# Attention output projection: plain fp32 products in place of three products of split halves

## What is computed

```python
def _L0_attn_ref(x, Wq, Wk, Wv, Wo):
    ...
    attn = jax.nn.softmax(scores, axis=-1).astype(x.dtype)
    ctx = jnp.einsum('bhgtk,bhkd->bhgtd', attn, v)
    out = ctx.reshape(b, H, t, DH).transpose(0, 2, 1, 3).reshape(b, t, E)
    return out @ Wo.T
...
h = _layernorm(x, axis=-1) * (1 + ca) + sa
x = x + ga * _L0_attn_ref(h, L0_attn_Wq, L0_attn_Wk, L0_attn_Wv, L0_attn_Wo)
h = _layernorm(x, axis=-1) * (1 + cb) + sb
x = x + gb * _L0_ffn_ref(h, ...)
```

## Time and profile before

| | |
|---|---|
| median of 3 runs | 870.54 us (870.29 to 873.26) |
| the profiled execution | 873.01 us |
| its span, first to last instruction | 871.0 us |
| PE busy | 750.3 us (86%), 4006 matmul records |
| DVE busy | 524.8 us (60%) |
| ACT busy | 331.0 us (38%) |
| POOL busy | 245.9 us (28%) |
| mean granted TensorE clock | 0.939 |

### The profile page before, as it was taken

How to read it: one execution, slowest core, us unless ns; L and a number is a source line. 1 busy time by engine, 2 the same in 40 slices (tenths; PEclk the granted TensorE clock), 3 DMA queues, 4 the chain that set the end, 5 groups by cost and what they waited for, 6 DMA issues and landing times.

```text
span 871.0 us, 11789 instructions
## 1 busy us (share of the span) xinstructions
PE 750.3 (86%) x4006; PEld 479.6 (55%) x4006; DVE 524.8 (60%) x761; ACT 331.0 (38%) x545; POOL 245.9 (28%) x189
## 2 busy tenths in 40 slices
PE   3678599999999999879799999667767799997998
PEld 1555333343333333228568888445546588885886
DVE  4757876767766767306745547998798433335410
ACT  6221046555655656762225400334421333222200
POOL 2445561200000000251246532373523222222500
PEclk9779779999999999999989999978798899999999
DMA  9047794610010110211013200210031021011110
GB/s 313 11 100 118 158 174 111 86 63 31 30 62 0 62 62 1 89 39 60 1 49 98 71 1 1 67 37 0 6 71 61 0 73 38 34 48 49 61 60 37
DMA packets 24379, 52.91 MB, mean 61 GB/s; under 512 B 4017, under 2 KB 8857, under 8 KB 23321
## 3 DMA queue, kind: packets, MB, share of 16 engines
q1 hardware_dynamic: 24345, 52.46, 23.1%
HBM read 45.63 MB, written 6.62 MB: 60 GB/s over the span
## 4 chain that ended last, share of the span: by engine, by line
PE 69%; DVE 19%; issue 5%; POOL 3%; ACT 3%; DMA 1%; SPq 0%; ACTq 0%; DVEq 0%; POOLq 0%
PE ps L841 67%; DVE mxp L1700 4%; DVE arena L1596 2%; DVE xnb L1584 2%; DVE arena L1593 1%; ACT pr L1399 1%; DMA wm<-in_wm 1%; DVE st L1566 1%; DVE rt L1900 1%; PE ps L858 1%; PE ps L1000 1%; DVE yz L1937 0%; POOL rs L2085 0%; ACT full L1293 0%; DVE x L1906 0%
## 5 line engine op out<-in xcount | busy, mean ns | idle before, releaser
L841 PE MATMUL ps<-arena 128*128 128x512 f32 (+1 forms) x1728 | 428.1, 409 | 47.8 <-DVE arena L1596 25.1
L841 PEld LDWEIGHTS ps<-arena 128*128 128x128 f32 (+1 forms) x1728 | 335.8, 196 | 130.1 <-issue 30.2
L1700 DVE TENSOR_REDUCE mxp<-ps 128x2 f32<-128x1024 f32 (+3 forms) x160 | 173.0, 1116 | 69.2 <-PE ps L841 68.4
L1399 ACT ACTIVATE pr<-ps 128x512 f32<-128x512 f32 x288 | 161.8, 596 | 124.8 <-PE ps L841 122.2
L841 PE MATMUL ps<-Kst,Qst 96*128 (+4 forms) x384 | 102.7, 339 | 11.5 <-DVE mxp L1700 5.8
L841 PE MATMUL ps<-Qst,Kst 99*128 (+1 forms) x288 | 105.6, 388 | 7.5 <-ACT pr L1399 4.3
L841 PEld LDWEIGHTS ps<-Kst,Qst 96*128 (+1 forms) x384 | 36.4, 100 | 75.3 <-issue 34.2
L841 PE MATMUL ps<-pr,vr 128*32 128x512 f32 x576 | 76.7, 605 | 0.7 <-ACT pr L1399 0.7
L841 PE MATMUL ps<-maskb,identb 128*128 128x128 bf16 (+1 forms) x320 | 75.5, 258 | 0.0
L841 PEld LDWEIGHTS ps<-Qst,Kst 99*128 (+1 forms) x288 | 27.2, 98 | 76.7 <-ACT pr L1399 49.8
L2168 POOL COPY vr<-vtok 128x128 f32 (+1 forms) x8 | 2.4, 294 | 205.9 <-PE ps L841 205.9
(11 more groups left out here) (180 smaller groups left out, 737.9 us busy)
## 6 DMA issues: line engine op xcount, KB each, us to landing
wmr<-in_wmr SPq DMA_DIRECT2D x8, 1280.0 KB, 5.5
raw<-in_w SPq DMA_DIRECT2D x16, 512.0 KB, 3.3
Qst<-q_parts SPq DMA_DIRECT2D x18, 256.0 KB, 8.9
q_parts<-qparts SPq DMA_DIRECT2D x3, 768.0 KB, 8.3
x<-in_x SPq DMA_DIRECT2D x8, 256.0 KB, 6.1
wm<-in_wm SPq DMA_DIRECT2D x4, 512.0 KB, 7.8
raw<-in_up SPq DMA_DIRECT2D x8, 256.0 KB, 2.5
raw<-in_down SPq DMA_DIRECT2D x8, 256.0 KB, 2.6
```

Of the source, the lines that this page charges most:

```text
L841: return nc.tensor.matmul(outp, lhs, rhs, start=start, stop=stop, skip_group_check=True)
L1399: A(pr[:, k % PRING, :], ps[:, 4 + k % 2, :], ACT.Exp, scale=float(DH) ** -0.5).then_inc(exp_done, 1)
L1700: V.tensor_reduce(mxp[:, kh, g0:g0 + heads, i].rearrange("p (b e) -> p b e", e=per), units, AXX, ALU.max)\
```

## The change

The transposed context is kept as one fp32 tile `aT`, and the weights as one fp32 tile `Wo`. ACT copies each bank into `aT`, and that copy now releases the bank. DVE's eight subtractions are gone. POOL writes chunk times gate row straight to `Wo`, without the rounding and the subtraction. PE makes one plain fp32 product per chunk where it made three of halves.

```diff
-        Wo = [ar(WR_W + 32 * K, KC, D), ar(WR_W + 40 * K, KC, D)]
+        Wo = at("Wo", [P, KC, D], F32, WR_B + 32 * 1024)
...
-        aTr = [ar(ACT_W, KC, T), ar(ACT_W + 16 * K, KC, T)]
+        aT = at("aT", [P, KC, T], F32, ACT_B)
...
                 for kc in range(KC):
-                    last = mm3(ps[:, b, :], hilo(aTr, lambda h: h[:, kc, tl(t)]), hilo(Wo, lambda w: w[:, kc, :]),
-                               kc == 0, kc == KC - 1)
+                    last = mm(ps[:, b, :], aT[:, kc, tl(t)], Wo[:, kc, :], kc == 0, kc == KC - 1)
...
             for hf in range(2):
                 for c in range(KC):
-                    split_hi(("aT", hf, c), aTr[0][:, c, tok[hf]])
+                    b = filled(act, ("aT", hf, c))
+                    A(aT[:, c, tok[hf]], ps[:, b, :], ACT.Copy).then_inc(read_b[b], 1)
...
-            for hf in range(2):
-                for c in range(KC):
-                    split_lo(n, ("aT", hf, c), aTr[0][:, c, tok[hf]], aTr[1][:, c, tok[hf]])
-                    n += 1
...
                 r = raw[:, piece_slot(("wo", k)), D * half:D * half + D]
-                link(nc.gpsimd.tensor_tensor(r, r, gabc[:, :], ALU.mult))
-                split(("wo", k), D, Wo[0][:, j, :], Wo[1][:, j, :], loaded=True, last=half == 1, at=D * half)
+                ins = nc.gpsimd.tensor_tensor(Wo[:, j, :], r, gabc[:, :], ALU.mult)
+                if half == 1:
+                    ins.then_inc(piece_done, 1)
```

## The result

In 17 runs each, the changed kernel took 878.43 us in the median (873.45 to 879.76), the kernel before 871.63 us (869.29 to 873.85). The ratio is 1.0063, with a 95% interval of 1.005 to 1.0076: 5.5 us slower, and between 4.4 and 6.6. The 5.5 us are the distance of the means (877.28 and 871.82 us); the medians lie 6.8 us apart, since the changed runs fall into two groups, six from 873.45 to 875.54 us at a mean granted clock of 0.943 to 0.947 and ten from 877.76 to 879.76 us at 0.934 to 0.942, and the median lies in the upper one. The profiled execution took 876.65 us, its span is 874.8.

A forecast was written before the change was run, and what follows sets the result against it. PE was taken to bound the stage almost alone; +5.7 us for products, -0.5 and -0.4 for two waits gave +4.8, so 870.54 became 875.3 us, range 872.6 to 878.9.

The forecast's parts named there:

- rival 2: Whole kernel: one or two more half-clock stretches come, +1.6 us each, giving 876.4 to 878.5 us; chance 0.17.
- Price of a record: PE's plain fp32 products: each leaves two records streaming for 0.43 us each, bounds 0.425 and 0.538.
- upper bound of 0.538: Time per fp32 record in us if the wait for weights stays with every record.
- The term +5.7: Products of the stage on PE: 64 records of 0.43 are 27.5 us in place of 21.8.
- rival 3: Products of the stage: each takes more than two records' time; four turns at 0.227 give 876.9 us; chance 0.10.
- Its other case: Products of the stage: weight wait in every record, 64 x 0.538 = 34.4 us, giving 882.3 us; within chance 0.10.
- First joint: Start of the products behind the first transposes: no wait for DVE's fourth subtraction, -0.5 us (bounds 0 and -0.5).
- Second joint: Behind tile 5, ahead of the transposes: PE's wait for the layer norm goes, -0.4 us.
- Sum: Whole kernel: +5.7 - 0.5 - 0.4 = +4.8 us, from 870.54 to 875.3 us, slower by 0.55%.
- What I costed at nothing: DVE's subtractions (4.88 us), POOL's eight instructions (7.6 us), layer norms behind tiles 3 and 7: hidden, no new wait.
- rival 1: Behind the stage: clock falls at 434.0 and 447.6 don't come, saving up to 3.2 us, 872.1 us; chance 0.18.
- My signs of being wrong: Adds every 2.7 or 4.3 us, granted clock falling inside the stage, or up loop's start shifted by other than 4 to 6 us.

The follow-up runs named there:

- the relief alone: Kernel before with its 96 fp32r products, but no lo halves made (no DVE subtractions, no POOL rounding or subtraction); ratio 1.0004, 872.53 us beside 872.45.

## Why the prediction was right

The time, 878.43 us, lies in the range of 872.6 to 878.9, and the ratio in the case with the largest chance, slower by over 0.5%. The interval begins just at 0.5%, so how near the line it would be was right too. In part that was luck. The time is 3.1 us above my 875.3, outside my forecast's own range of 874.2 to 876.4, and in the band of rival 2 (876.4 to 878.5, chance 0.17), whose mechanism the traces do not show. What was right by its mechanism is the stage. Point by point:

- **What bounds the stage**: PE, from the transposes to the second half's layer norm. Shown: the chain after is almost all PE, and the relief alone is worth 0.60 us.
- **Price of a record**: forecast 0.43 from one isolated product; measured 0.429 in the stream and 0.430 for each added one. Taking off both the wait for the first weights and the way through the array was right; the upper bound of 0.538 is out. The term +5.7 is 64 x 0.429 - 96 x 0.227 = +5.7.
- **Four turns at the fp32r pace** (rival 3): out for the change. With four products of halves a tile takes 3.63 us, with plain ones 3.43. The price of that rival was right: 32 x 0.227 = 7.3 us. (Its other case has a slip: 34.4 - 21.8 is 12.6, not 12.7.)
- **First joint**: forecast -0.5; -0.51 in the trace (392.12 - 388.57 = 3.55 against 4.06), -0.59 with fp32r products.
- **Second joint**: forecast -0.4; all 0.55 us between the end of six tiles of 2.72 and the transposes went, since the transposes now start 20.61 us behind the first product, which is 48 x 0.429.
- **Sum**: forecast +4.8, measured +4.55 in three traces. The term that was mis-sized is the second joint, by 0.15; some 0.1 more lies in the starts at the changes from one kind of product to the next.
- **What I costed at nothing**: the subtractions, POOL's work, the layer norm behind tile 3 and behind tile 7. No new wait appeared.
- **The clock** (rivals 1 and 2): the falls are real, and rival 1 is out, since the fall behind the long wait is in all ten traces that don't fill it. That rival 2's further falls came with the change is not shown: at this place the clock is half for 6.9 us in place of 6.8, and the mean granted clock over the runs is 0.940 in place of 0.941. The price of a fall is not one number: I took 1.6 us, and against the 8.42 us of the 36 records at full clock it costs 1.3 to 2.5 us (9.75 to 10.95), more where more of the half-clock time falls on the records (3.19 us of it in the first trace of before, 4.87 in the first changed one). My own range had room for half a stretch only downwards; with it upwards too it would have ended at 877.2, and one whole stretch puts rival 2 at 876.9 and not 876.4.
- **Why 875.3 lies 3.1 us too low**: 1.1 us of it is the base. I took +4.8 onto 870.54, the median of three runs, and 17 runs give 871.63; the sentence of rival 2, that this median was lucky, was right. The other 2.0 us are the medians' distance of 6.8 us in place of 4.8. By the means it is 5.5, which leaves 0.9 over the stage in these runs and 0.7 over all. Two stretches of the traces, ahead of the stage and in the tail, each vary by over 2 us between executions of one kernel. Whether the later tail is also in truth longer by 0.7 us after the change stays open.
- **My signs of being wrong**: the adds came every 3.43 us, and the clock stayed full in the stage. The start of the up loop moved by 2.7 us and not by 4 to 6, by the timelines of PE up to 460 us, before and after:

```profile
446.25 13.94 PE L841 MATMUL ps<-arena 128*128 128x512 f32 x53 [1.61 <-POOL arena L2066]
```

```profile
448.99 11.27 PE L841 MATMUL ps<-arena 128*128 128x512 f32 x48 [1.61 <-POOL arena L2062]
```

Taken as written, that sign says that I was wrong. But these starts hold the 2.5 us by which this execution was ahead when the stage began, which I had not thought of. Counted from the first transposes the loop starts after 60.4 us in place of 55.2, which is 5.3 later; the other traces have 60.3 and 59.7 changed, 56.2 before.

## What to carry to other kernels

On a stage bound by TensorE, count what the array streams: with 128 x 512 at full clock a plain fp32 product costs 0.86 us and three fp32r products cost 0.68, so dropping the halves pays only where making them costs the critical path more than 0.18 us a product; here it was 0.02 (0.60 us over 32 products). Price a shape that the kernel has only in isolation by its start-to-start time, less the first wait for weights, and check by doubling it. Where executions differ by several us, measure the changed stage between two fixed instructions of the trace, and give the whole only the interval that many runs allow.

## What was not expected of the hardware

Sixteen spare products that compute nothing kept the clock up right behind the wait: the 36 records there took 8.4 us in place of 9.75 to 10.95, and the tail was 1 to 5 us shorter than in the unfilled traces of the same kernel. In the changed kernel a fall of 3.4 us came at the start of the up loop all the same. And with the same program on PE ahead of the stage, it began between 387.6 and 392.0 us in the fourteen traces, a spread about as large as the whole effect of the change.
